# The second half of a fused block, rewritten as one instruction stream with routing by scatter

## The reference, cut to what matters

```python
x2 = x1 + gate0 * y[first expert] + gate1 * y[second expert]   # what the first part ends with
z  = (x2 - mean) / sqrt(var + eps)                             # no gain, no bias
shared = (gelu(z @ w1s) * (z @ w2s)) @ w3s                     # 256 -> 1024 -> 256, every token
e  = argmax(z @ Wg)                                            # one of 8 experts a token
routed = (gelu(z @ W1[e]) * (z @ W2[e])) @ W3[e]               # same shape, that expert's weights
out = x2 + shared + routed
```

## Time and profile before

| | |
|---|---|
| median of 3 runs | 974.52 us (973.53 to 974.78) |
| the profiled execution, its own time | 966.43 us |
| its span (first to last recorded instruction) | 964.7 us |
| PE busy | 858.3 us, 89% |
| DVE, ACT, POOL busy | 46%, 33%, 36% |
| first part ends (PE's last matmul) | 484.7 us |
| routed tiles | about 680 to 937 us |

### The profile page before, as it was taken

The page is one execution under the profiler, slowest core; times in us unless marked ns, Lnnn a source line. Parts: engine busy times, 40 slices in busy tenths (PEclk is TensorE's granted clock), DMA queues, the critical chain, the costliest instruction groups (busy, mean ns, idle before and its releaser), DMA issues. The chain is left out here.

```text
span 964.7 us, 19179 instructions
## 1 busy us (share of the span) xinstructions
PE 858.3 (89%) x6306; PEld 768.6 (80%) x6306; DVE 445.0 (46%) x1253; ACT 316.3 (33%) x712; POOL 349.3 (36%) x605
## 2 busy tenths in 40 slices
PE   5899989886667999999949999968999999999994
PEld 4567766665566889999849999957999999999993
DVE  1279989888774555555523333353111111111113
ACT  1466767664542445555411111100111111111110
POOL 1445677766775355544142222211100010000006
PEclk9899999998688989999979999989999999999998
DMA  9875557534612322263121111102998988999716
GB/s 355 277 268 189 194 112 233 155 103 188 169 43 53 79 67 83 83 214 84 50 66 33 34 38 40 38 28 73 336 330 305 329 301 324 303 319 306 270 61 175
DMA packets 92096, 161.79 MB, mean 168 GB/s; under 512 B 13832, under 2 KB 71112, under 8 KB 88680
## 3 DMA queue, kind: packets, MB, share of 16 engines
q1 hardware_dynamic: 71008, 103.39, 32.2%
q10 hardware_dynamic: 12832, 37.82, 10.5%
q0 software_dynamic: 8176, 19.57, 7.9%
HBM read 146.10 MB, written 14.66 MB: 167 GB/s over the span
## 5 line engine op out<-in xcount | busy, mean ns | idle before, releaser
L1691 PEld LDWEIGHTS bank<-zT_f,we 128*128 128x128 f32 x1472 | 167.9, 192 | 1.8 <-ACT zT_f L1979 0.7
L1691 PE MATMUL bank<-zT_f,we 128*128 128x128 f32 x1472 | 168.2, 275 | 0.5 <-ACT zT_f L1979 0.5
L1708 DVE TENSOR_TENSOR hT_f<-bank,act_g 128x512 f32<-128x512 f32 x78 | 53.8, 691 | 227.6 <-PE bank L1691 208.0
L1700 ACT ACTIVATE act_g<-bank 128x512 f32<-128x512 f32 x78 | 46.6, 597 | 320.4 <-PE bank L1691 320.4
L1691 PE MATMUL bank<-zT_c,a_x 128*128 128x128 f32 x1024 | 121.4, 281 | 0.3 <-PEq L1521 0.3
L1691 PEld LDWEIGHTS bank<-zT_c,a_x 128*128 128x128 f32 x1024 | 119.2, 197 | 0.8 <-issue 0.7
L361 POOL DMA_INDIRECT arena_a<-rows_e,pick x78 | 76.0, 975 | 29.8 <-issue 29.8
L410 PE MATMUL bank<-arena_b,arena_a 128*128 128x128 f32 x624 | 81.8, 288 | 1.6 <-DVE hT L546 1.6
L1715 PE MATMUL bank<-we,hT_f 128*128 128x256 f32 x368 | 83.2, 379 | 0.0
L410 PEld LDWEIGHTS bank<-arena_b,arena_a 128*128 128x128 f32 x624 | 78.2, 204 | 2.4 <-DVE arena_b L538 2.4
L1715 PEld LDWEIGHTS bank<-we,hT_f 128*128 128x128 f32 x368 | 68.1, 190 | 8.3
(11 more groups left out here) (273 smaller groups left out, 1361.8 us busy)
## 6 DMA issues: line engine op xcount, KB each, us to landing
we<-in_W_dram SPq DMA_DIRECT2D x69, 1024.0 KB, 7.4
arena_a<-in_ctx_n_dram ACTq DMA_DIRECT2D x16, 1152.0 KB, 7.2
arena_a<-in_ctx_t_dram SPq DMA_DIRECT2D x16, 1028.0 KB, 9.0
rows_y<-arena_a ACTq DMA_DIRECT2D x39, 128.0 KB, 1.7
arena_a<-in_w_moe_dram ACTq DMA_DIRECT2D x3, 1156.0 KB, 5.3
arena_a<-in_w_moe_dram ACTq DMA_DIRECT2D x3, 1152.0 KB, 7.5
rows_f<-yr ACTq DMA_DIRECT2D x23, 128.0 KB, 6.3
rows_e<-arena_b SPq DMA_DIRECT2D x64, 32.0 KB, 4.0
```

What stands on the lines that cost most here:

```text
L1691: last = nc.tensor.matmul(bank[half][:, f * P:(f + 1) * P], w12[:, i, k, col0:col0 + P], zT[:, k], start=k == 0, stop=k == KD - 1)
L1700: nc.scalar.activation(act_g[:, half], bU[half][:], ACT.Gelu).then_inc(self.ac_g, 1)
L1708: nc.vector.tensor_tensor(hT[:, parity, half * HH:(half + 1) * HH].rearrange("p f t -> p (f t)"), bG[half][:], act_g[:, half], ALU.mult).t ...
```

## The change

Both parts become one block. The second part is written out without loops, as five lists (`part2_sync`, `part2_pool`, `part2_tensor`, `part2_scalar`, `part2_vector`), each called right after the first part's list of that engine. Each list runs over 39 **slots**; in each slot PE does `hidden` of one unit and `down` of the unit before. The helpers `Step`, `sweep`, `routing`, `Geglu` and the semaphore clearing between blocks go away.

- Chunks are combined in 9 groups: two of one chunk, seven of two. In slot i PE also computes the ranks of group i (between the two halves of `hidden`) and the transposes and router scores of group i + 1.
- Routing follows the first part's manner: per group DVE takes the largest score, PE the ranks, DVE the place in the list, POOL scatters token numbers to `tab_f` in DRAM (one indirect DMA a chunk). After the last group DVE computes the tile map; SP then loads W1, W2 of tile 0 and fetches the 23 tiles' entries, one DMA each.
- The order of units is 11 shared, routed tile 0, shared 11, routed tiles 1 to 22, shared 12 to 15.
- The final gathers take three semaphore counts (10, 4 and 2 chunks); the last chunk's shared result is added last.
- Buffers: gathers go straight from `slot1`, without the copy to `pick_c`; all 16 chunks of `ya`, `yb` and the transposed chunks are kept; three buffers for the gathered tile rows instead of four.
- In the first part: some semaphores are merged; the waits on a tile's list entries are grouped otherwise (`PICKED`); the list `tab_f` is zeroed by one more DMA; POOL's constants for the old routing are replaced by three instructions; the gelu table is loaded in advance.

The diff, cut to its core:

```diff
-            with nc.Block() as block:            # (three more blocks, loops by sweep)
...
+        GROUPS = [(0, 1), (1, 2)] + [(c, c + 2) for c in range(2, G, 2)]
+        SLOTS = ([("s", c) for c in range(NGR + 2)] + [("r", 0), ("s", NGR + 2)]
+                 + [("r", n) for n in range(1, NT2)] + [("s", c) for c in range(NGR + 3, G)])
...
+        def part2_sync(sp):
+            for c in range(G):
+                sp.wait_ge(c_dv_z, c + 1)
+                sp.dma_start(rows_z[c * P:(c + 1) * P, :], z4[:, c]).then_inc(c_put, 16)
...
+            def pick_rows(n):
+                at = sp.value_load(place2[0:1, n:n + 1], min_val=0, max_val=T_ROWS // P - 1)
+                sp.dma_start(pick2[:, n], tab_f[bass.ds(at * P, P), :]).then_inc(f_pick, 16)
+            sp.wait_ge(c_dv_map, 1)
+            load_w12(0)
+            sp.wait_ge(c_po_tab, 16 * G)
+            for n in range(NT2):
+                pick_rows(n)
+            for n in range(1, NT2):
+                load_w12(n)
+                load_w3(n - 1)
...
+        def part2_pool(pool):
...
+            for i in range(-1, NGR):
+                if i + 1 < NGR:
+                    rstd(i + 1)
+                if i + 3 < NGR:
+                    gather_sums(i + 3)
+                if i >= 0:
+                    list_rows(i)
+            pool.wait_ge(c_put, G * 16)
+            pool.wait_ge(f_pick, 16 * NT2)
+            for n in range(NT2):
+                gather_tile(n)
...
+        def part2_tensor(pe):
...
+            for i in range(NSLOT):
+                hidden(i, 0)
+                if i < NGR:
+                    ranks(i)                      # waits for largest(i) on DVE
+                hidden(i, 1)
+                if i + 1 < NGR:
+                    transposed(i + 1)
+                if in_slot(i + 1, "r") is not None:
+                    transpose_z(in_slot(i + 1, "r"))
+                if i > 0:
+                    down(i - 1)
+                if i + 1 < NGR:
+                    router(i + 1)
+            down(NSLOT - 1)
...
+        def part2_scalar(act):
...
+            for i in range(NSLOT):
+                gelu(i, 0)
+                store(i - 2)
+                gelu(i, 1)
...
+        def part2_vector(dve):
...
+            for i in range(NSLOT):
+                if i >= 2:
+                    take(i - 2)                   # waits for down(i - 2) on PE
+                if i + 1 < NGR:
+                    combine(i + 1)
+                if i < NGR:
+                    largest(i)
+                products(i, 0)
+                if i == NSLOT - 1:
+                    finish(1)
+                if i < NGR:
+                    places(i)
+                if i + 1 < NGR:
+                    normed(i + 1)
+                if i == NGR - 1:
+                    tile_map()
+                products(i, 1)
+                if i == NGR:
+                    row_numbers()
+                if i == NSLOT - 2:
+                    finish(0)
+            take(NSLOT - 2)
+            finish(2)
+            dve.drain()
+            take(NSLOT - 1)
...
-            if n < NM:
-                return m_pick[n], 16
-            if TA <= n < TA + NM:
-                return m_pick[NM + n - TA], 16
-            return m_pick[2 * NM + n // NM], 16 * NM
+            for i, (lo, hi) in enumerate(PICKED):
+                if lo <= n < hi:
+                    return m_pick[i], 16 * (hi - lo)
```

More of the change, by code:

```diff
@@ L18 @@
 R_LOW = 52.0
[L21 to L48, removed]
 def need(eng, sem, value):
@@ L309, in perceiver_block @@
         TA = 9
+        PICKED = ((0, 1), (1, 2), (2, 3), (3, 6), (6, TA), (TA, TA + 1), (TA + 1, TA + 2), (TA + 2, TA + 6), (TA + 6, TA + 15), (TA + 15, NT1))
+        m_pick = [sem1(f"m_pick{i}") for i in range(len(PICKED))]
         assert 2 * CUT - E + 1 >= TA
@@ L489, in step @@
                     for k in range(2):
-                        nc.scalar.activation(gate[:, k], lead[:], ACT.Sigmoid, scale=1.0 - 2.0 * k)
+                        last = nc.scalar.activation(gate[:, k], lead[:], ACT.Sigmoid, scale=1.0 - 2.0 * k)
+                    last.then_inc(m_gate, 1)
             return step
@@ L609, in mix_sync @@
             sp.dma_start(ws3, w3s.rearrange("(f p) d -> p f d", p=P)).then_inc(ld_s, 16)
-            for i in range(NM):
-                sp.wait_ge(m_put[i], NT1 // NM * 16)
         def mix_pool(pool):
@@ L1464, in mix_vector @@
                 moe(m)
+        GROUPS = [(0, 1), (1, 2)] + [(c, c + 2) for c in range(2, G, 2)]
+        NGR = len(GROUPS)
+        NT2 = (TOK - E) // P + E
+        SLOTS = ([("s", c) for c in range(NGR + 2)] + [("r", 0), ("s", NGR + 2)]
+                 + [("r", n) for n in range(1, NT2)] + [("s", c) for c in range(NGR + 3, G)])
+        NSLOT = len(SLOTS)
+        assert NSLOT == G + NT2
+        UNIT_R = [SLOTS.index(("r", n)) for n in range(NT2)]
+        UNIT_S = [SLOTS.index(("s", c)) for c in range(G)]
@@ new lines, in perceiver_block @@
+        HH = HC // 2
+        NF, NZ = 2, NM
+        rows_z = nc.dram_tensor("rows_z", [TOK, D], F32).ap()
+        rows_f = nc.dram_tensor("rows_f", [NT2 * P, D], F32).ap()
+        in_a = Carve(arena_a, FLOATS_A)
+        we12 = in_a.take(NF, 2 * KD * H).rearrange("p w (i k h) -> p w i k h", i=2, k=KD)
+        we3 = in_a.take(NF, HC, D)
+        ya, yb = (in_a.take(G, D) for _ in range(2))
+        in_b = Carve(arena_b, FLOATS_B)
+        zT_c = in_b.take(G, KD, P)
+        hT_f = in_b.take(2, HC, P)
@@ new lines, in perceiver_block @@
+        act_g = in_b.take(2, HH * P)
+        zr, z4, yg = in_b.take(NZ, D), ya, x1
+        zT_f, yr = in_b.take(NF, KD, P), in_b.take(NF, D)
+        bZ, bU, bG, bY, bL = banks[0], banks[1:3], banks[3:5], banks[5:7], banks[7]
+        g_pe_u, g_pe_g, g_pe_y, g_ac_g, g_dv_h, g_dv_y = sems1("g_pe_u g_pe_g g_pe_y g_ac_g g_dv_h g_dv_y")
+        c_put = sem1("c_put")
+        c_pe_z, c_pe_l, c_pe_rank, c_ac_z, c_ac_lg = sems1("c_pe_z c_pe_l c_pe_rank c_ac_z c_ac_lg")
+        c_dv_var, c_dv_z, c_dv_mask, c_dv_prod, c_dv_slot, c_dv_map, c_dv_row = sems1(
+            "c_dv_var c_dv_z c_dv_mask c_dv_prod c_dv_slot c_dv_map c_dv_row")
@@ new lines, in perceiver_block, with counted_on @@
+        c_po_r, c_po_tab = sems1("c_po_r c_po_tab")
+        f_pick, f_sum, f_out = sems1("f_pick f_sum f_out")
+        Y_PARTS = ((0, 10), (10, 14), (14, G))
+        def counted_on(sems, parts, first, sizes):
+            count = list(first)
+            for i, n in enumerate(sizes):
+                count[i % parts] += 16 * n
+                yield sems[i % parts], count[i % parts]
+        after_moe = [NT1 // NM * 32] * NM
+        got_all = list(counted_on(m_got, NM, after_moe, [2 * (hi - lo) for lo, hi in GROUPS] + [1] * NT2))
@@ new lines, in perceiver_block @@
+        got_sum, got_tile = got_all[:NGR], got_all[NGR:]
+        after_tiles = [max(v for s, v in got_all if s is m) for m in m_got]
+        got_y = list(counted_on(m_got, NM, after_tiles, [hi - lo for lo, hi in Y_PARTS]))
+        got_w12 = list(counted_on(ld_kt, NF, [len(range(i, G, N3)) * 16 for i in range(NF)], [2] * NT2))
+        got_w3 = list(counted_on(ld_ctx, NF, [len(range(i, G, N3)) * 16 for i in range(NF)], [1] * NT2))
+        put_tile = list(counted_on(m_put, NF, [NT1 // NM * 16] * NF, [1] * NT2))
@@ L1469, in _ @@
                 mix_sync(sp)
+                part2_sync(sp)
             @block.gpsimd
@@ L2034, in laid_out @@
+                part2_vector(dve)
 def laid_out(inputs):
```

839 lines of the change are left out of this document (320 added, 519 removed).

## The result

| | before | changed |
|---|---|---|
| median of the runs | 974.28 us (973.53 to 974.78) | 1000.84 us (999.12 to 1001.22) |
| profiled execution, its span | 966.43, 964.7 | 1000.57, 998.8 |
| predicted | | 967.0, span 957.2 |

What follows compares the result with a forecast made beforehand. PE's own work was taken as the bound: 39 units, 413.4 us. With added work, waits and ending, 460.8 us from the first unit at 496.4 gave span 957.2, execution 958.9, plus 8.1 carried over: 967.0 us, range 954 to 974.

Steps and rivals of the forecast that it cites:

- constant 8.1: Whole kernel: the runs' median lies 8.1 us above the profiled execution, unexplained, carried over from 958.9 to 967.0.
- Start: Second part's start: without the all-engine meeting and the copy, first unit at 496.4, 2.4 us earlier, bounds -4 to 0.
- Tile slots: Routed tiles: same loads and waits per tile, slots 10.8 us apart with no idle.
- ending: After tile 22: final gathers vanish behind four shared units; PE's last down, one add and one store leave 2.8 us.
- Cold start: First hidden of the second part: takes 8.85 us after a stretch at granted clock 0.50, costing 1.7 us.
- A new wait in slots 2 to 7: Combining slots: PE waits 1.3 us before ranks for DVE's largest, 7.8 us, plus 0.4 in slot 1.
- Another new wait, before tile 0: Before tile 0: 23 list entries at 1.126 us delay the gather; PE stands 15.7 us, bounds 11.9 to 18.
- restart: PE after the wait before tile 0: a cooled down takes 5.36 us for 3.46, costing 1.9.
- Landed by about 9.7: Slot 8, list scatter: POOL scatters two chunks by 7.8 us, landed by about 9.7 us into the slot.
- the slots' group work: Combining slots on PE: pairs' transposes and scores 8.0 us, group 1's unhidden copy 1.4, ranks 2.7.
- Rival C: Slots from 11 on: straight-line code starves PE's instruction fetch; at 0.75 us per slot 21.0 us more, 988; chance 0.10.
- 8.4 us of a 13.3 us slot: it hides: Combining slots, POOL: 4 gathers, 2 scatters and a root take 8.4 us per slot and cost nothing.

Runs made afterwards that it cites:

- stand-in: Changed kernel with the last gathers, from the fifth on, each waiting for the landing of the one four before; at the upper level 965.55 us beside 967.04, 0.9989 of before.

## Why the prediction was wrong

Its trace and its runs were of two levels, and I carried the difference over as a constant 8.1 us. The two have to be compared apart: the miss of 33.8 us is 5.3 in the stand-in's span at the trace's level, plus 36.3 between the levels, less the 8.1 carried over, within 0.4.

*At the level of the trace* the stand-in's span is 962.5 for the predicted 957.2; 0.9989 of before for 0.992, so the forecast gain is missing there too.

- Start: first unit at 497.71, predicted 496.4, within its bounds. Tile slots of 10.82 us, ending (2.5 us from the last `take`): right. Cold start: the first `hidden` took 10.0 us for my 8.85 (6.3 and 3.65 for its halves).
- *A new wait in slots 2 to 7*: right in kind, mis-sized. PE waits 0.58 to 0.94 us ahead of the ranks, ended by DVE's last `earlier`; all slots 4.2, not 8.2. In the stand-in's slot 2 DVE needs 5.0 us from its `take` to the end of the last `earlier` (520.88 to 525.88) for my 5.3, and PE reaches its ranks 4.6 us after the `down` (scores at 520.67, half a `hidden` to 525.31) for my 4.3; the wait is the small difference of the two.
- *Another new wait, before tile 0*: this is the step that failed at this level. 20.45 us for 15.7, above my upper bound of 18, and 2.2 for the restart. The entries' cadence (24.92 - 0.34) / 22 = 1.117 us and the gather behind them (33.5 us from SP's first entry to PE, predicted 33.2) were right. "Landed by about 9.7" was not: I gave the scatter of the list the 1.8 us of a plain transfer. From its issue at 629.24 to SP's release it took 9 us, 638.43; and 9 us too where no weight load stood beside it (617.80 less 608.75 in the variant with the first entries first). There the raw trace has the 32 landing records of the last two scatters spread from 609.44 to 617.00. SP's first entry is 15.9 us into slot 8 for my 11.2: 4.7 us, the whole miss of that step. The Trainium skill says of a DMA's completion signal that it can bring "a surprisingly long delay especially when the write target is HBM" (DMA: Bandwidth & Descriptors, "Anatomy of one DMA — SWDGE (gpsimd) path"); by that rule, which I hadn't weighed, the trace agrees in the length of the wait, for this scatter if not for the plain stores to HBM of 1.7 us; whether the signal or the writing of 128 short rows takes the time, no run separates.
- Of the 5.3 the start makes 1.3; the rest, about 3 us, is the cold start's 1.1 and the slots' group work, some 0.3 us in each of slots 2 to 7.

*At the level of the runs* the changed kernel's span is 36.3 us above the stand-in's at the other level. By the intervals between takes: first unit and first part 4.7, slots 2 to 4 1.3, 8.6 and 0.4, slot 5 8.2, slot 37 with 38 12.9, before tile 0 0.3: 36.4. No step of the prediction has this: it put the effect of POOL's gathers on the other engines at nothing. Rival C had its shape (PE gets one instruction per 0.7 us or more) and is wrong as a mechanism: it put 0.75 us into each of 28 slots, and the tile slots show none; it forecast the stalls under a full DMA load, and they come with DMA at 0.17 to 0.28; and halving POOL's last gathers, which leaves PE's program as it was, removed the stall beside them. My sentence on POOL, "8.4 us of a 13.3 us slot: it hides", was right for POOL's time and missed what its gathers do to the others; with the constant 8.1 it is the step that failed at this level.

So the ending, on which the change was to win, is the one place where it lost most: it moved a row of sixteen gathers from a place where PE was done to a place beside PE's last units. Before pays 2.1 to 2.9 us for it at the lower level, the changed kernel 12.9. What was shown: the stalls belong to the code and the level together (same file, 962.5 and 992.3), the last one goes when the row is spaced to 3.1 us or cut to eight. Not shown: that the 18.4 us in slots 2 to 5 have the same cause, since no run changed the gathers there at the lower level (their look, PE's steps and "remote" beside a close row, is the same); why one row of six issues stalls PE by 8 us and the next doesn't; and what a level is.
## What to carry to other kernels

Runs far from the profiled execution of the same kernel are a second condition, not an offset: take a trace at each before a forecast is a few per cent deep. Long close rows of gathers by GpSimd should lie where nobody waits for a signal; a shorter row helped here at one place (eight for sixteen), while rows of six still went with 8 us elsewhere, and spacing them cost more than it gave. "It hides" needs a look at the other engines' signals as well as at the issuing engine's time. When a list is fetched entry by entry, fetch first what the next engine wants, and give a scatter its own measured landing, not a plain transfer's.

## What the runs showed of the hardware

- A scatter of 128 short rows by GpSimd released its waiter 7.7 to 10.0 us after its issue (two in a row, 1.27 us apart, the last of sixteen, in 16 traces), a gather of 128 rows of 1 KB some 3 us after (2.04 to 2.32 us from the end of the issue, in the spaced variant).
- Landing records in the raw traces, as a count over all of them: at the upper level 7996 to 8014 of 8080 (before) and 8433 to 8554 of 8592 to 8720 (changed and variants); at the lower 6269, and 6311 to 6725. Few are missing in the stretch of the tiles (1470 to 1474 for 1488 over 19 units in the traces counted); in the ending 440 to 447 are left of the upper level's 637 to 639 with sixteen close gathers, and 615 with the same sixteen spaced to 3.1 us. So records are lost where signals are held up, and both go away with spacing; whether the recorder is part of the cause stays open: no run without it was compared.
- PE's granted clock was 0.84 in the stalled slots 3 and 5 and 1.00 in slot 4, and the first `down` behind 20.55 us of idle took 5.92 us for 3.62, the one behind 4.27 us 6.32.
